# A chain of four graph layers on one core: the two tables that PE reads before each four edge steps joined in one

## The chip, the cores and the metric

The kernel runs on one core of a Trainium2 chip. The metric is the device time of one execution in microseconds (us). Three timed executions took 4398.54, 4406.31 and 4406.6 us; the median is 4406.31 us.

## The reference, cut to what matters

50000 nodes of 128 values pass through four graph layers, with a residual and a layer normalisation after each. There are 25000 edges, sorted by `dst`; `dst` is dense at low node numbers (a uniform draw squared), `src` is uniform. The core of each layer is a sum over edges:

```python
# l0, twice: messages weighted by the edge, summed by dst, averaged, two products, leaky relu
agg = jax.ops.segment_sum(x[src] * ew[:, None], dst, num_segments=n) + x
# l1: rows of dst summed by src
msg_sum = jax.ops.segment_sum(x[col] @ W_msg + b_msg, row, num_segments=n)
# l2: edge attributes summed by dst
aggregated = jax.ops.segment_sum(edge_attr, dst, num_segments=num_nodes)
# l3, twice: rows reflected at a relation's unit vector, summed by dst
h_ref = h_src - 2.0 * dot * h_rel
out = jax.ops.segment_sum(h_ref, tgt, num_segments=x.shape[0])
```

## The kernel before

A front part sorts the edges by their `dst` and by their `src` node and makes tables of the order in which the sums are taken. Then five edge stages, `l0a`, `l0b`, `l1`, `l3a` and `l3b`, alternate with five node stages. All engines meet between two stages (`stage_end`, `stage_begin`).

The nodes stand in 98 groups of 512 (`GROUPS`), the sorted edges in 196 tiles of 128 (`TILES`). A sum over edges is a product: the tile's 128 gathered rows against a matrix of ones and zeros (`hit`, 128 x 512) that says which of the 512 nodes each edge belongs to. A tile whose edges reach over a border of groups takes one step in each of its groups, so a stage has 293 steps (`STEPS`). Rows are split in three bf16 parts (`got`, `rest`, `tail`), so a step is three multiplications (L1554), and in `l0a`, where the edge attributes of `l2` are summed beside, six. Four banks of PSUM hold four groups; ACT copies a finished group out (L1316), clears its bank (L1301) and stores the sums.

The work of a stage runs on all engines at once. POOL gathers rows in batches of four tiles into a ring of sixteen (L719) and waits, before it fills a place again, for the step that last read it, a number that it loads from `ring_tab` (L712). DVE weighs or reflects the rows, splits them (L1103, L1106), and makes the hits (L1071) up to a hundred steps ahead. PE multiplies. Which tile and which group a step has depends on the data, so PE reads them from tables that the front part wrote in SBUF. Steps go in quads of four; there are 74 (`FOURS`). For each quad PE's queue reads eight words of `step_tab` (L1534): four places in the ring and four banks. For every other quad it reads four words of `wait_tab` (L1540): for each of two quads, how many batches of messages must be ready and how many banks cleared. These are masked (L1563, L1564) and waited for, together with the count of hits. Then the quad's steps follow, each with register operations for its addresses (L1554, in PE's queue) ahead of its weight loads and multiplications. The loads for the next quad stand in the queue behind the last multiplication of a quad and before the waits of the next. The order is written out in the program, without a loop:

```python
of = numbers(step_tab, q + 1, 0, 2 * K)      # eight words
if q % 2:
    waits = waits_of(q + 1)                  # four words
```

The tables are filled on DVE in `step_tables` and cleared before (L1011, L1012).

Of the kernel before, what the change touches and what calls it, by code (L numbers as in the profile page):

```python
# [8 lines left out]
I32 = mybir.dt.int32  # L9
U16 = mybir.dt.uint16  # L10
ALU = mybir.AluOpType
ACT = mybir.ActivationFunctionType
AX_X = mybir.AxisListType.X
PE_ENGINE = mybir.EngineType.PE
# [9 lines left out]
K = 4  # L24
ROWS = K * P
GROUPS = -(-N // ROWS)
LAST_NODES = (N - (GROUPS - 1) * ROWS) // K
XROWS = GROUPS * ROWS
TILES = -(-E // P)
FULL_PARTS = E // TILES  # L30
REST = E - FULL_PARTS * TILES
BATCHES = TILES // K
STEPS = GROUPS + TILES - 1
FOURS = -(-STEPS // K)
# [16 lines left out]
IN_RANGE = "the table is built on the chip from counts of tiles and groups, which bound it"  # L51
# [39 lines left out]
def program(nc, t, out):  # L91

    ctx = ExitStack()
    with ctx:
        def sb(name, shape, dt=F32):
            return ctx.enter_context(nc.sbuf_tensor(name, shape, dt))
# [62 lines left out]
        sorted_by = {"dst": sb("sorted_by_dst", [P, TILES, FIELDS], I32)}  # L159
        node_at = {n: sb(f"node_at_{n}", [P, STEPS]) for n in ("dst", "src")}  # L160
        link3 = sb("link3", [3 * K + 3, 8, P], BF16)
        step_tab = {n: sb(f"step_tab_{n}", [1, FOURS, 2 * K], I32) for n in ("dst", "src")}
        wait_tab = {n: sb(f"wait_tab_{n}", [1, FOURS, 2], I32) for n in ("dst", "src")}
        group_tab = {n: sb(f"group_tab_{n}", [1, 104], I32) for n in ("dst", "src")}
        ring_tab = {n: sb(f"ring_tab_{n}", [1, 56], I32) for n in ("dst", "src")}

# [37 lines left out]
        tab_i = front("tab_i", [1, 4, STEPS + 3], I32)  # L204
# [225 lines left out]
        def stage_begin(engine, n):  # L430

            engine.wait_ge(s_stage, ENGINES * n)
# [380 lines left out]
        def _(dve):  # L813
# [126 lines left out]
            def step_tables(name):  # L940

                n = SORTS.index(name)
                dve.tensor_copy(end_row_i[:, :], total_row[name][:, :])
                dve.tensor_copy(end_col_i[:, :], total_col[name][:, :])
                dve.drain()
                dve.tensor_scalar(end_row_i[:, :], end_row_i[:, :], 7, None, ALU.arith_shift_right)
                dve.tensor_scalar(end_col_i[:, :], end_col_i[:, :], 7, None, ALU.arith_shift_right)
                dve.drain()
                dve.tensor_copy(end_row_f[:, :], end_row_i[:, :])
                dve.tensor_copy(end_col[:, 0:1], end_col_i[:, :])  # L950
                dve.drain()
                dve.scalar_tensor_tensor(out=group_tab[name][:, 0:GROUPS], in0=end_row_f[:, :], scalar=1.0, in1=iota_t[0:1, 0:GROUPS],
                                         op0=ALU.add, op1=ALU.add)
                dve.tensor_tensor(end_col[:, 1:2], end_col[:, 0:1], iota_p[0:GROUPS, 0:1], ALU.add)
                dve.tensor_scalar(past_ring[:, 0:BATCHES], iota_t[0:GROUPS, K - 1:K - 1 + TILES:K], end_col[:, 0:1], None, ALU.is_ge)
                dve.drain()
                dve.tensor_scalar(past[:, :], iota_t[0:GROUPS, :], end_col[:, 1:2], None, ALU.is_gt)
                dve.drain().then_inc(s_tab1, 1)
                dve.wait_ge(s_tab2, n + 1)
                dve.tensor_copy(group_at[name][:, :], ps[:, 7, 0:STEPS + 3])  # L960
                dve.tensor_tensor(ring_tab[name][:, 0:BATCHES], ps[0:1, 7, STEPS + 3:STEPS + 3 + BATCHES], iota_t[0:1, K:K + TILES:K], ALU.add)
                dve.drain()
                dve.tensor_tensor(tile_at[:, :], iota_t[:, :], group_at[name][:, :], ALU.subtract)
                dve.drain()
                dve.tensor_scalar(pick0[name][:, :], tile_at[:, 0:STEPS], iota_p[:, 0:1], None, ALU.is_equal)
                dve.tensor_scalar(pick1[name][:, :], tile_at[0:TILES - P, 0:STEPS], iota_p[0:TILES - P, 1:2], None, ALU.is_equal)
                dve.tensor_copy(tab_i[:, 0, :], tile_at[0:1, :])
                dve.tensor_copy(tab_i[:, 1, :], group_at[name][0:1, :])
                dve.drain()
                dve.tensor_scalar(tab_i[:, 2, :], tab_i[:, 0, :], RING - 1, None, ALU.bitwise_and)  # L970
                dve.tensor_scalar(tab_i[:, 3, :], tab_i[:, 0, :], 2, None, ALU.arith_shift_right)
                dve.tensor_scalar(wait_tab[name][:, :, 1], tab_i[:, 1, K - 1:STEPS + 3:K], 1, GROUPS, ALU.add, ALU.min)
                dve.drain()
                dve.tensor_scalar(wait_tab[name][:, :, 0], tab_i[:, 3, K - 1:STEPS + 3:K], 1, BATCHES, ALU.add, ALU.min)
                dve.tensor_copy(step_tab[name][:, :, 0:K], tab_i[:, 2, :].rearrange("a (q j) -> a q j", j=K))
                dve.tensor_scalar(tab_i[:, 0, :], tab_i[:, 1, :], BANKS - 1, None, ALU.bitwise_and)
                dve.drain()
                dve.tensor_copy(step_tab[name][:, :, K:2 * K], tab_i[:, 0, :].rearrange("a (q j) -> a q j", j=K))
                dve.drain()
# [28 lines left out]
            for name in SORTS:  # L1008
                dve.memset(ring_tab[name][:, :], 0)
                dve.memset(group_tab[name][:, :], 0)  # L1010
                dve.memset(step_tab[name][:, :, :], 0)  # L1011
                dve.memset(wait_tab[name][:, :, :], 0)  # L1012
            step_tables("dst")
            dve.wait_ge(s_win, 16 * len(small_loads))
            dve.wait_ge(s_comb, 1)
# [414 lines left out]
        def _(pe):  # L1430
# [66 lines left out]
            def keys_of_tiles(name):  # L1497

                n = SORTS.index(name)
                pe.wait_ge(s_tab3, 2 * n + 1)  # L1500
                pe.transpose(ps[:, 6, 0:P], keys_s[:, 0:P], ident[:, :])
                pe.transpose(ps[0:TILES - P, 6, P:2 * P], keys_s[:, P:TILES], ident[:, :]).then_inc(s_tab4, 1)
# [25 lines left out]
            def edges(name, n):  # L1528
                stage_begin(pe, n)
                s = edge_s[name]  # L1530
                by = WINDOWS[name][0]
                def numbers(table, q, lo, hi):

                    return nc.values_load_multi_w_load_instructions(  # L1534
                        table[by][0:1, q, lo:hi], engines=[PE_ENGINE], min_val=0, max_val=TILES,
                        skip_runtime_bounds_check_because=IN_RANGE)[1]

                def waits_of(q):

                    return nc.values_load_multi_w_load_instructions(  # L1540
                        wait_tab[by][0:1, q:q + 2, :].rearrange("a q f -> a (q f)"), engines=[PE_ENGINE], min_val=0, max_val=TILES,
                        skip_runtime_bounds_check_because=IN_RANGE)[1]

                w = BUFFERS[name]

                def products(i, slot, bank):

                    slot = nc.s_assert_within(slot, 0, RING - 1, skip_runtime_bounds_check_because=IN_RANGE)
                    bank = nc.s_assert_within(bank, 0, BANKS - 1, skip_runtime_bounds_check_because=IN_RANGE)
                    for h in range(1 + w.pair):  # L1550
                        into = ps[:, BANKS * h:BANKS * h + BANKS, :][:, bass.ds(bank, 1), :].rearrange("p a n -> p (a n)")
                        for part in (w.got_hi[h][:, bass.ds(slot, 1), 1:2 * D:2], w.rest_hi[h][:, bass.ds(slot, 1), 1:2 * D:2],
                                     w.tail[h][:, bass.ds(slot, 1), 0:D]):
                            last = pe.matmul(into, part.rearrange("p a d -> p (a d)"), w.hit[:, i % w.hits, :], start=False, stop=False,  # L1554
                                             skip_group_check=True)
                    last.then_inc(s["step"].sem, 1)

                waits = waits_of(0)
                of = numbers(step_tab, 0, 0, 2 * K)
                for q in range(FOURS):  # L1560
                    ready, clear = waits[2 * (q % 2):2 * (q % 2) + 2]
                    pe.wait_ge(*s["hit"](min(K * q + K, STEPS)))
                    pe.wait_ge(s["msg"].sem, ready & 63)  # L1563
                    pe.wait_ge(s["zero"].sem, clear & 127)  # L1564
                    for j in range(min(K, STEPS - K * q)):
                        products(K * q + j, of[j], of[K + j])
                    if q + 1 < FOURS:
                        of = numbers(step_tab, q + 1, 0, 2 * K)
                        if q % 2:
                            waits = waits_of(q + 1)  # L1570
                if name == "l0b":
                    keys_of_tiles("src")

# [182 lines left out]
            def nodes(phase):  # L1756
                phase()
                stage_end(pe)

            edges("l0a", 1)  # L1760
            nodes(d0)
            edges("l0b", 2)
# [32 lines left out]
```

## Time and profile before

| | us |
|---|---|
| median of three timed runs | 4406.31 |
| span of the profiled execution | 4783.9 |
| busy: PE, DVE, POOL, ACT | 3733.3, 3413.8, 2954.6, 2211.2 |
| `l0a`, from 528 to 944 | 416 |
| `l0b`, from 1277 to 1604 | 327 |
| `l1`, from 2002 to 2333 | 331 |
| `l3a`, from 3309 to 3658 | 349 |
| `l3b`, from 3988 to 4336 | 348 |

The times come from runs without a profile; the span is that of one execution under the profiler, from its first instruction to its last, and the only time that is given for that execution. It is 377.6 us above the median. The stretches of the edge stages are read from the times at which L1534 and L1554 start and end; they hold the first waits of a stage and the last stores of the one before. PE's queue (PEldq in the rows) is the engine's own sequence of instructions: register operations and table loads stand there and are not counted as busy time, and the engine's multiplications (PE) and weight loads (PEld) are issued from it.

### The profile page before, as it was taken

How to read it: one execution, taken by the hardware profiler on the slowest of the kernel's cores; microseconds unless marked ns; L12 is line 12 of the kernel's file. 1: busy time of each engine (PE TensorE's matmuls, PEld its weight loads, DVE VectorE, ACT ScalarE, POOL GpSimd, SP SyncE). 2: the span in 40 equal slices, each digit the busy share in tenths (PEclk: the TensorE clock that was granted, in tenths of full speed). 3: DMA queues.
4: the chain of work that ended last, by engine and by line, in shares of the span. 5: the costliest groups of instructions: out<-in, count | busy, mean ns of one | idle time of the engine just before them, and what ended most of it. 6: DMA issues, size and time to landing. Idle time of an engine off the chain costs nothing.

```text
span 4783.9 us, 90087 instructions
## 1 busy us (share of the span) xinstructions
PE 3733.3 (78%) x18662; PEld 2281.7 (48%) x18662; DVE 3413.8 (71%) x13249; ACT 2211.2 (46%) x4608; POOL 2954.6 (62%) x3411
## 2 busy tenths in 40 slices
PE   2155799998778999777899999995678774778776
PEld 1012344477523455422598888894224442234443
DVE  5338965355665577743498988897877888768898
ACT  0000046733225688633366666664145652256666
POOL 4650355366566699866466666664665776656787
PEclk6556899999889999889899999997899997999999
DMA  3340157777524788534555555552456773467776
GB/s 88 99 74 6 53 173 222 251 230 232 168 86 159 246 259 271 175 124 130 170 166 161 167 162 161 161 168 66 122 180 227 235 234 113 147 194 246 226 238 194
DMA packets 536159, 810.98 MB, mean 170 GB/s; under 512 B 129245, under 2 KB 184005, under 8 KB 535709
## 3 DMA queue, kind: packets, MB, share of 16 engines
q1 hardware_dynamic: 318844, 532.13, 35.3%
q10 hardware_dynamic: 162769, 169.41, 10.5%
q0 software_dynamic: 54096, 104.47, 8.0%
q8 instruction: 157, 2.57, 0.2%
q14 instruction: 293, 2.40, 0.2%
HBM read 493.49 MB, written 311.41 MB: 168 GB/s over the span
## 4 chain that ended last, share of the span: by engine, by line
PE 47%; DVE 19%; issue 14%; DVEq 6%; POOL 6%; DMA 3%; another core or an unknown queue 2%; ACT 1%; POOLq 0%; ACTq 0%; SPq 0%; PEldq 0%
PE ps L1554 18%; DVEq L68 5%; DVE stat L1122 4%; PE ps L1719 4%; PE ps L1700 4%; PE ps L1701 4%; DVE hit L1071 3%; PE ps L1487 3%; POOL got L719 2%; PE ps L1679 2%; POOL x2T L734 2%; PE ps L1710 2%; PE ps L1680 2%; DVE mv L1128 2%
## 5 line engine op out<-in xcount | busy, mean ns | idle before, releaser
L754 POOL TENSOR_TENSOR rstd<-vare,neg_half 128x4 f32<-128x4 f32 x686 | 710.3, 1035 | 430.6 <-DVE vare L1135 429.6
L1554 PE MATMUL ps<-hit,got 128*128 128x512 bf16 x1172 | 492.5, 420 | 381.7 <-issue 155.9
L1316 ACT ACTIVATE evac<-ps 128x512 f32<-128x512 f32 x392 | 233.4, 595 | 861.8 <-PE ps L1554 625.3
L719 POOL DMA_INDIRECT got<-nodes_l,sorted_by_dst x392 | 398.2, 1016 | 239.5 <-PE ps L1554 109.8
L1554 PE MATMUL ps<-hit,tail 128*128 128x512 bf16 x1172 | 490.2, 418 | 22.8 <-issue 20.8
L1554 PE MATMUL ps<-hit,rest 128*128 128x512 bf16 x1172 | 491.9, 420 | 20.2 <-issue 18.9
L1163 DVE TENSOR_TENSOR nT<-sums,ps 128x512 f32<-128x512 f32 x392 | 268.9, 686 | 270.8 <-PE ps L1599 100.3
L1301 ACT ACTIVATE ps<-zeros 128x512 f32<-128x512 f32 x588 | 344.3, 598 | 195.0 <-DVEq L428 170.1
L1554 PEld LDWEIGHTS ps<-hit,got 128*128 x1172 | 121.8, 104 | 649.3 <-issue 566.0
L719 POOL DMA_INDIRECT got_pair<-in_x,sorted_by_dst x196 | 203.5, 1038 | 363.5 <-DVEq L428 190.1
L669 POOL DMA_INDIRECT records_by_src<-record,place_src x196 | 201.1, 1026 | 162.0 <-PE ps L1587 90.6
L1338 ACT ACTIVATE aff<-ps,shift,rstd 128x128 f32<-128x128 f32 x784 | 290.6, 448 | 22.1 <-POOL shift L757 22.1
L1736 PE MATMUL ps<-xin,ident 128*128 128x512 f32 x392 | 218.4, 640 | 84.3 <-DVE nT L1163 84.3
L719 POOL DMA_INDIRECT got<-nodes_c,sorted_by_dst x196 | 195.0, 995 | 134.1 <-PE ps L1554 72.7
L1071 DVE TENSOR_SCALAR hit<-node_of,node_at_dst 128x512 bf16<-128x512 f16 x879 | 260.0, 364 | 11.5 <-SPq L428 11.1
L1348 ACT ACTIVATE xT<-ps 128x512 f32<-128x512 f32 x294 | 175.0, 596 | 196.7 <-PE ps L1666 159.4
L719 POOL DMA_INDIRECT got<-nodes_a,sorted_by_src x196 | 195.1, 996 | 108.0 <-issue 53.7
L1740 PEld LDWEIGHTS ps<-w_r,nT 128*128 128x128 f32 x1568 | 211.8, 196 | 98.5 <-issue 98.5
L1103 DVE TENSOR_TENSOR rest<-got 128x512 f32<-128x512 f32 x196 | 136.1, 694 | 171.8 <-DMA got<-nodes_a,sorted_by_src 116.9
L1128 DVE BATCH_NORM_AGGREGATE mv<-stat 128x2 f32<-128x6 f32 x2744 | 230.3, 155 | 34.3 <-issue 1.9
L669 POOL DMA_INDIRECT records_by_dst<-row,place_dst x196 | 191.5, 977 | 101.7 <-issue 101.7
L743 POOL TENSOR_TENSOR aff<-aff,g 128x512 f32<-128x512 f32 x196 | 248.6, 1268 | 4.4 <-issue 2.9
(276 smaller groups left out, 10298.4 us busy)
## 6 DMA issues: line engine op xcount, KB each, us to landing
nodes_l<-xout SPq DMA_DIRECT2D x196, 256.0 KB
xin<-nodes_l SPq DMA_DIRECT2D x196, 256.0 KB
sums<-sums_l SPq DMA_DIRECT2D x196, 256.0 KB
sums_l0a<-evac_pair ACTq DMA_DIRECT2D x98, 256.0 KB
sums_l<-evac_pair ACTq DMA_DIRECT2D x98, 256.0 KB
sums<-sums_l0a SPq DMA_DIRECT2D x98, 256.0 KB
sums_l0b<-evac ACTq DMA_DIRECT2D x98, 256.0 KB
sums<-sums_l0b SPq DMA_DIRECT2D x98, 256.0 KB
```

What stands on the lines that cost most here:

```text
L68: engine.drain()
L669: pool.indirect_dma_start(out=rec_d[name], out_offset=bass.IndirectOffsetOnAxis(ap=place[name][:, k:k + 1], axis=0), in_=of(k), in_offset= ...
L719: pool.indirect_dma_start(out=BUFFERS[name].got[0][:, k % RING, :], out_offset=None, in_=table, in_offset=bass.IndirectOffsetOnAxis(ap=sor ...
L743: pool.tensor_tensor(aff[:, slot, :, :], aff[:, slot, :, :], g3[:, layer:layer + 1, :].to_broadcast([P, K, D]), ALU.mult).then_inc(s["scal ...
L754: pool.tensor_tensor(rstd[:, n, at, :], vare[:, n, at, :], neg_half[:, :], ALU.pow)\
L1071: dve.tensor_scalar(hit[:, i % HITS, :], node_of[:, :], node_at[by][:, i:i + 1], None, ALU.is_equal)\
L1128: dve.bn_aggr(mv[:, n, slot % 4, k, :], stat[:, n, k, :])
L1163: dve.tensor_tensor(nT[:, slot % 4, :], sums[:, slot, :], ps[:, bank + slot % banks, :], ALU.mult).then_inc(s["nT"].sem, 1)
L1301: last = act.activation(ps[:, BANKS * h + g % BANKS, :], zeros[:, :], ACT.Copy)
L1316: act.activation(w.evac[h][:, slot, :], ps[:, BANKS * h + g % BANKS, :], ACT.Copy).then_inc(s["out"].sem, 1)
L1338: last = act.activation(dest[:, slot % ring, k, :], rows[:, slot % rows.shape[1], k, :], ACT.Identity, bias=shift[:, n, at, k:k + 1], scal ...
L1554: last = pe.matmul(into, part.rearrange("p a d -> p (a d)"), w.hit[:, i % w.hits, :], start=False, stop=False, skip_group_check=True)
```

## The change

The four words of `wait_tab` move into `step_tab`: its row of a quad has twelve words instead of eight, of which ten are used, four places, four banks and the quad's own two wait values. PE reads these ten in one load for each quad. `wait_tab` and its clearing are gone; DVE writes the two wait values to columns 9 and 8 of the new rows with the same instructions. The waits, their values and their place ahead of a quad stay as they were.

```diff
-        step_tab = {n: sb(f"step_tab_{n}", [1, FOURS, 2 * K], I32) for n in ("dst", "src")}
-        wait_tab = {n: sb(f"wait_tab_{n}", [1, FOURS, 2], I32) for n in ("dst", "src")}
+        step_tab = {n: sb(f"step_tab_{n}", [1, FOURS, 3 * K], I32) for n in ("dst", "src")}
...
-                dve.tensor_scalar(wait_tab[name][:, :, 1], tab_i[:, 1, K - 1:STEPS + 3:K], 1, GROUPS, ALU.add, ALU.min)
-                dve.drain()
-                dve.tensor_scalar(wait_tab[name][:, :, 0], tab_i[:, 3, K - 1:STEPS + 3:K], 1, BATCHES, ALU.add, ALU.min)
+                dve.tensor_scalar(step_tab[name][:, :, 2 * K + 1], tab_i[:, 1, K - 1:STEPS + 3:K], 1, GROUPS, ALU.add, ALU.min)
+                dve.drain()
+                dve.tensor_scalar(step_tab[name][:, :, 2 * K], tab_i[:, 3, K - 1:STEPS + 3:K], 1, BATCHES, ALU.add, ALU.min)
...
                 dve.memset(step_tab[name][:, :, :], 0)
-                dve.memset(wait_tab[name][:, :, :], 0)
...
-                def numbers(table, q, lo, hi):
+                def numbers(q):
 
                     return nc.values_load_multi_w_load_instructions(
-                        table[by][0:1, q, lo:hi], engines=[PE_ENGINE], min_val=0, max_val=TILES,
-                        skip_runtime_bounds_check_because=IN_RANGE)[1]
-
-                def waits_of(q):
-
-                    return nc.values_load_multi_w_load_instructions(
-                        wait_tab[by][0:1, q:q + 2, :].rearrange("a q f -> a (q f)"), engines=[PE_ENGINE], min_val=0, max_val=TILES,
+                        step_tab[by][0:1, q, 0:2 * K + 2], engines=[PE_ENGINE], min_val=0, max_val=TILES,
                         skip_runtime_bounds_check_because=IN_RANGE)[1]
...
-                waits = waits_of(0)
-                of = numbers(step_tab, 0, 0, 2 * K)
+                of = numbers(0)
                 for q in range(FOURS):
-                    ready, clear = waits[2 * (q % 2):2 * (q % 2) + 2]
+                    ready, clear = of[2 * K:2 * K + 2]
...
                     if q + 1 < FOURS:
-                        of = numbers(step_tab, q + 1, 0, 2 * K)
-                        if q % 2:
-                            waits = waits_of(q + 1)
+                        of = numbers(q + 1)
```

## Rows read from the trace of the kernel before

**Rows 1.** Page, parts 1 and 3: busy us of each engine; a queue's packets, MB.

```profile
PE 3733.3 (78%) x18662; PEld 2281.7 (48%) x18662; DVE 3413.8 (71%) x13249; ACT 2211.2 (46%) x4608; POOL 2954.6 (62%) x3411
...
q8 instruction: 157, 2.57, 0.2%
```

**Rows 2.** Page, part 4: the chain that ended last, by engine and by line.

```profile
PE 47%; DVE 19%; issue 14%; DVEq 6%; POOL 6%; DMA 3%; another core or an unknown queue 2%; ACT 1%; POOLq 0%; ACTq 0%; SPq 0%; PEldq 0%
PE ps L1554 18%; DVEq L68 5%; DVE stat L1122 4%; PE ps L1719 4%; PE ps L1700 4%; PE ps L1701 4%; DVE hit L1071 3%; PE ps L1487 3%; POOL got L719 2%; PE ps L1679 2%; POOL x2T L734 2%; PE ps L1710 2%; PE ps L1680 2%; DVE mv L1128 2%
```

**Rows 3.** Windows: length, busy us of PE, PEld, DVE, ACT, POOL; clock, DMA, GB/s.

```profile
528.00:944.00 416.00, 388.16 (x1769) 174.41 (x1767) 245.49 (x539) 215.56 (x392) 204.01 (x197) 0.97 0.62 195
1277.00:1604.00 327.00, 236.14 (x895) 92.82 (x895) 186.01 (x443) 117.75 (x199) 200.60 (x197) 0.86 0.41 136
...
3309.00:3658.00 349.00, 239.53 (x892) 93.64 (x892) 251.77 (x981) 116.35 (x196) 195.00 (x196) 0.85 0.50 157
```

**Rows 4.** PE's weight loads in time, `l0b`: start us, us; idle us before and releaser.

```profile
1529.53 0.10 PEld L1554 LDWEIGHTS ps<-hit,got 128*128 x1 [0.52 <-issue]
...
1530.01 0.10 PEld L1554 LDWEIGHTS ps<-hit,got 128*128 x1
...
1531.72 0.10 PEld L1554 LDWEIGHTS ps<-hit,tail 128*128 x1
1532.72 0.10 PEld L1554 LDWEIGHTS ps<-hit,got 128*128 x1 [0.90 <-issue]
```

**Rows 5.** PE's register operations by line, `l0b`: count, then ns minimum/median/maximum.

```profile
L1563 PEldq ALU_OP  x74: 3/36/709, 1280.1 to 1600.1; - x74
...
L1564 PEldq ALU_OP  x74: 2/32/708, 1291.0 to 1600.2; - x74
...
L1554 PEldq FUSED_REGOPS  x586: 3/37/1393, 1291.1 to 1600.7; - x196
```

**Rows 6.** Chain by line in 1400:1604, 2045:2333, 3430:3658 and 4108:4336 us.

```profile
by line: PE ps L1554 47.0%; issue 19.6%; POOL got L719 7.5%; DMA got<-nodes_l,sorted_by_dst 7.1%; DMA sums_l0b<-evac 6.8%; ACT evac L1316 3.0%; DVE hit L1071 1.8%; DVE tail L1106 1.7%; DVE got L1085 1.7%; DVE rest L1103 1.7%; ACT ps L1301 1
...
by line: PE ps L1554 53.5%; issue 24.5%; POOL got L719 11.7%; DMA got<-nodes_a,sorted_by_src 5.1%; DVE hit L1071 1.5%; DVE tail L1106 1.4%; DVE rest L1103 1.4%; POOLq L712 0.2%; ACT evac L1316 0.2%; PE ps L1676 0.1%; PE ps L1679 0.1%; POOLq
...
by line: PE ps L1554 50.6%; issue 19.0%; DMA got<-nodes_c,sorted_by_dst 6.9%; POOL got L719 4.7%; ACT evac L1316 3.4%; ACT ps L1301 2.6%; DVE hit L1071 2.4%; DVE prod L1091 2.3%; DVE got L1096 2.3%; DVE rest L1103 1.8%; DVE tail L1106 1.0%;
...
by line: PE ps L1554 46.6%; issue 18.5%; DMA got<-nodes_l,sorted_by_dst 11.6%; POOL got L719 5.8%; DVE hit L1071 3.7%; DVE prod L1091 3.1%; DVE got L1096 3.1%; DVE rest L1103 2.4%; DVE tail L1106 1.3%; DVEq L1099 0.9%; POOLq L712 0.8%; ACT 
```

**Rows 7.** Table loads by line: PE's of eight, of four words, then ACT's.

```profile
L1534 PEldq TENSOR_LOAD <-step_tab_dst x296: 3/592/1931, 530.3 to 4331.6; - x148
...
L1540 PEldq TENSOR_LOAD <-wait_tab_dst x148: 3/334/1022, 529.7 to 4328.8; - x148
...
L1309 ACTq TENSOR_LOAD <-group_tab_dst x100: 304/312/694, 529.7 to 4331.7; - x100
```

**Rows 8.** What PE idled for before L1554, `l0a` whole, then from 600 us: us, times.

```profile
  issue: 40.1, 41
...
  issue: 6.3, 9
```

**Rows 9.** Loads of four words in the late stretches of `l0b`, `l1`, `l3b`.

```profile
L1540 PEldq TENSOR_LOAD <-wait_tab_dst x26: 328/334/707, 1404.0 to 1596.7; - x26
...
L1540 PEldq TENSOR_LOAD <-wait_tab_src x34: 13/334/712, 2045.7 to 2324.9; - x34
...
L1540 PEldq TENSOR_LOAD <-wait_tab_dst x28: 4/392/955, 4115.2 to 4328.8; - x28
```

**Rows 10.** POOL's gathers, 1400 to 1604 us: busy us, mean ns; idle before by releaser.

```profile
L719 POOL DMA_INDIRECT got<-nodes_l,sorted_by_dst x116 | 119.5, 1030 | 63.2 <-PE ps L1554 32.0 <-issue 31.1
```

**Rows 11.** Clearing of `step_tab` on DVE.

```profile
L1011 DVE MEMSET step_tab_dst<- x1: 552/552/552, 192.4 to 192.4; 1x592 int32 x1
```

**Rows 12.** PE's weight loads in time in a slow stretch of `l0b`.

```profile
1427.05 0.10 PEld L1554 LDWEIGHTS ps<-hit,rest 128*128 x1 [1.23 <-issue]
```

## The prediction

> **What bounds the kernel now.** I read the page first, then the chain of waits, then each edge stage by windows, and last the instructions of PE's own queue. The page has PE busiest, 78% of a span of 4783.9 us, and DVE at 71% [rows 1]. A share that high on two engines says only that stages alternate, so the chain of what ended last is the next view: 47% of it is PE, 14% is "issue", and the longest single line is L1554, the edge products, with 18% [rows 2]. L1554 runs in five stretches: 416 us for `l0a`, and from 327 (`l0b`) to 349 us (`l3a`) for the four single stages [rows 3]. In `l0a` (two banks of products per step) PE is busy 388 of 416 us; in `l0b` it is busy 236 of 327 and in `l3a` 240 of 349 us, so there something else holds it. The change touches only what stands between two quads in these five stretches.
>
> What holds it is seen in the order of PE's weight loads around a quad boundary [rows 4]. Inside a quad they follow each other by 0.214 us (eight intervals from 1530.01 to 1531.72); a quad's first one comes after an idle gap of 0.52 us where one table load stands before it (1529.53) and of 0.90 us where two do (1532.72). The releaser is "issue": no semaphore was late, the queue was busy reading registers. The same shows in the waits' own instructions: L1563 and L1564, the masks of the wait values, which carry the waits, last 36 and 32 ns at the median [rows 5].
>
> That holds from about a third of each stage on. In `l0b` from 1400 us on L1554 and issue make 66.6% of the chain, and in the late stretches of `l1`, `l3a` and `l3b` 78.0, 69.6 and 65.1% [rows 6]. The quads before these stretches wait for their first messages, the late ones for PE's queue.
>
> **The change part by part.** *The price of a load.* A load of eight words lasts 592 ns at the median, one of four 334 ns [rows 7] (296 and 148 of them by the `dst` tables, and a quarter as many more by `src`). The difference, 258 ns for four words, is 64.5 ns a word, which leaves 334 - 4 x 64.5 = 76 ns that each load costs whatever its length. ACT's loads of four words, 312 ns, fit the same price [rows 7]. Between a load and the next instruction of the queue lie a further 58 ns: the second load adds 0.90 - 0.52 = 0.38 us to the gap [rows 4], and 0.38 is 0.334 with some 0.05 to 0.06 around it.
>
> *Removed*: 37 loads of four words in each of five stages, 185 in all. *Added*: two words to each of the 370 loads. Over two quads the words stay twenty (8 + 8 + 4, then 10 + 10), so what goes is one load's fixed part: 76 + 58 = 134 ns. By lengths: before 592 + 592 + 334 + 3 x 58 = 1692 ns, after 2 x (592 + 129 + 58) = 1558 ns. Every boundary then costs about 0.65 us of idle PE, where now 0.52 and 0.90 alternate.
>
> No load of ten words is in this trace. Bounds from the nearest rows: not under the 592 ns of eight words (then two quads would save 134 + 258 = 392 ns), and not over the price of an eight and a four one after the other, 592 + 334 = 926 ns (two quads then lose 276 ns). I take 721 ns, the line through both lengths, since both lie in one plain transfer of a row of the same tile and no row shows a step.
>
> *Where it counts.* In `l0a` a quad is 24 multiplications and PE's idle time there ahead of L1554 is 40.1 us by issue over the whole stage, but only 6.3 us from 600 us on [rows 8]; the loads run while the multiplications of the last quad still execute. I cost it at nothing there; with that cover gone it would be 37 x 0.134 = 5 us. In the early stretches of the other four the saved time turns into a longer wait for messages: nothing. In the four late stretches stand 26, 34, 28 (`l3a`, whose row is not shown) and 28 of the four-word loads [rows 6, 9], 116 in all: 116 x 0.134 = 15.5 us. Of these I count the share in which L1554 and issue are the chain, on the mean of the four 70% [rows 6]: 10.9 us. In the rest the ring of gathered rows, DVE's splitting or the stores of the sums are last, and follow PE only in part.
>
> *What is late next.* POOL gathers a batch ahead of PE. In `l0b`'s late 204 us it is busy 119.5 us and loses 31.1 to its own issue, 32.0 to PE [rows 10]; so the gathers could end some 32 us sooner if PE let them, nine times the 26 x 0.134 = 3.5 us that the change wants there.
>
> *No cost.* The clearing of two `wait_tab` goes, the clearing of the two `step_tab` grows from 592 to 888 words, at 552 ns for 592 by under 0.28 us each [rows 11]: at most 0.6 us in the front part, less what goes. The writes of the two columns are the same instructions to another stride. The waits keep their values and their places ahead of each quad; none is added, nothing is moved past another queue. The tables take 1184 bytes more of a partition (2 x 74 x 8), which shifts the buffers behind them and changes no access.
>
> *Fewer instructions.* PE's queue now and then crawls: around 1427 us a weight load inside a quad stands behind 1.23 us of idle time, one of four alike within six us, with issue as the releaser [rows 12], and register operations that take 37 ns at the median reach 1.4 us in that stage [rows 5]. The trace has 157 packets of 2.57 MB in an instruction queue [rows 1]. 185 fewer instructions can spare one such crawl, at most some 6 us; I leave it out of the sum and in the range. The Trainium skill (Runtime: NRT & Kernel Launch, section Instruction fetch mechanics) gives 16 KiB blocks of 256 instructions, which by it would be 0.7 of one block here; the trace's 2.57 MB over 157 packets agree with the block's size.
>
> The sum is made in the profiled execution, of which only the span is given, 4783.9 us, and that is 377.6 us above the median of the three timed runs, 4406.31. If the crawls belong to profiling, the timed run is nearer to the gathers' own pace and a part of the 10.9 us goes. If the late stretches shrink in proportion, the saving per load stays, since it is a fixed time of PE's queue. I keep 11 us: 4406.3 - 10.9 = 4395.4, say 4395.
>
> **The rivals.** *Hidden after all, no change.* Without crawls PE's queue needs 3.19 us from quad to quad with two loads (1529.53 to 1532.72) and 0.38 less, 2.81 us, with one [rows 4], 0.75 us a step, against 2.57 us of multiplications (12 x 0.214), while POOL needs 4 x (1.03 + 0.27) = 5.2 us for a batch of four tiles [rows 10]. A batch takes four to eight steps, so where fewer than 5.2 / 0.75, some seven, fall to it POOL or the DMAs set the pace, and what PE saves becomes its wait. For it: 377.6 us of the profile's span are not in the timed runs, and gathers stand in every late chain with 12 to 17%, DMA and POOL together [rows 6]. Against it: POOL's 32.0 us of waiting for PE. Price: 15.5 x 0.2 = 3 us gained, so 4401 to 4408.
>
> *The price lies in the words alone.* Then twenty words before and after cost the same: 4406. The two lengths speak against it: four words at 64.5 ns would be 258, not 334 ns. The Trainium skill (Runtime: NRT & Kernel Launch, section Instruction fetch mechanics) has such a rule, about 200 ns per register even in bulk, for register loads from HBM. These are from SBUF and the trace disagrees in size: 592 ns for eight where the rule would give 1600.
>
> *Slower: the long load has a step.* If a load over eight words is done as two reads, each boundary costs 926 ns instead of 592: a pair of quads rises from 1692 to 2 x (926 + 58) = 1968 ns, 276 ns more, and 116 of them 32 us: 4438. It decides from 1692/2 - 58 = 788 ns on, only 67 ns above my 721. For it: ten words and a stride of twelve are new here, the third length no row shows; loads already stretch at times, to 1931 ns at most [rows 7], and a longer one has more to be stretched. Against: the regular price of two lengths.
>
> **How the numbers follow.** The forecast's case (a fixed part goes, PE's queue is what is late) has 0.50, with its own range 4380 to 4400; hidden 0.30; words alone 0.07; the step or a stretched load 0.13, from 4410 up. Three timed runs spread over 8 us, so 0.2% (8.8 us) is about what can be told from no change. The forecast's case puts a few in a hundred within it, and hidden and words nearly all theirs: faster 0.47, same 0.39, slower 0.14. The low end is the 15.5 us in full, 7 us for the stretching that goes with the second load (its median in the last stage is 392 ns, not 334 [rows 9]) and one crawl of 6 us: 4378. The high end goes a quarter of the way into the step: 4413.
>
> **What would show it.** PE's queue with 370 loads of some 720 ns and none at `wait_tab`; gaps of 0.6 to 0.7 us ahead of every late quad; `l0a` as long as before; the four single stages each 2 to 5 us shorter; POOL's waits for PE down by as much. Wrong would be: loads of 790 ns or more; gaps gone but longer waits at L1563 or L1564; stages of one length while something outside of them moved.

## The result

The changed kernel takes 4418.57 us (median of five, 4413.81 to 4422.76) against 4403.33 us for the kernel before (five, 4393.41 to 4406.6): a ratio of 1.0039, interval 1.0026 to 1.0051. It is slower by 0.4%. I had forecast 4395 us, in a range of 4378 to 4413. Two executions of the later comparisons, one of before at 11224 us and one of the twelve-word kernel at 5523 us, are left out of their ratios.

The page of the profile after; PE is busy for 82% of a span shorter than that of [rows 1]:

```profile
span 4421.0 us, 89900 instructions
...
PE 3611.1 (82%) x18662; PEld 2252.9 (51%) x18662; DVE 3415.3 (77%) x13247; ACT 2213.6 (50%) x4608; POOL 2978.8 (67%) x3411
...
q8 instruction: 157, 2.57, 0.2%
...
PE 45%; DVE 18%; POOL 12%; issue 12%; DVEq 6%; DMA 5%; ACT 1%; POOLq 1%; ACTq 0%; SPq 0%
PE ps L1546 14%; DVEq L68 5%; POOL got L718 4%; DVE stat L1120 4%; PE ps L1708 4%; POOL records_by_dst L668 4%; PE ps L1689 4%; PE ps L1690 4%; DVE hit L1069 3%; PE ps L1668 2%; PE ps L1610 2%; PE ps L1609 2%; PE ps L1699 2%; PE ps L1669 2%; POOL x2T L733 2%
```

The span, 4421.0 us, agrees with the timed runs. That of the first profile of before, 4783.9 us, did not. Of [rows 1] the order of the engines stayed, PE and DVE busiest, and the 157 packets of code. So the kernel before was run and profiled once more.

**e0_before**, the same text as before.

> The kernel before once more, for a profile that stands nearer to its timed runs than the first one (span 4783.9 us against a median of 4403 us), whose PE queue crawled some sixty times. All theories expect a span of 4395 to 4410 us, loads of 592 ns (eight words) and 332 ns (four), and no register operation of L1554 over 0.6 us. Stages then: l0b 295 us, l1 280, l3a 305, l3b 305, each 3 to 6 us under the changed kernel's. If the crawls come back, they belong to the kernel and not to that one execution.

Measured: 4402.95 us, span 4401.1 us. The crawls of PE's queue did not come back: no register operation of the products takes more than 89 ns in this profile (L1554), nor more than 84 in the changed kernel's (L1546), where [rows 5] had up to 1393. The changed kernel's first mask of the wait values is its L1554. Columns as there; first before, with its loads of eight and of four words, then the changed kernel:

```profile
L1554 PEldq FUSED_REGOPS  x3223: 37/55/89, 388.6 to 3950.2; - x190
...
L1534 PEldq TENSOR_LOAD <-step_tab_dst x296: 587/592/1605, 375.6 to 3949.0; - x148
...
L1540 PEldq TENSOR_LOAD <-wait_tab_dst x148: 327/334/1027, 375.0 to 3946.2; - x148
```

```profile
L1554 PEldq ALU_OP  x370: 36/36/36, 375.6 to 3969.7; - x185
...
L1546 PEldq FUSED_REGOPS  x3223: 37/55/84, 387.9 to 3970.2; - x190
```

There are two levels. The first three comparisons had the kernel before near 4403 us, the four later ones had it at 4776 to 4819 us, as in the first profile. Within one comparison, which is on one chip, the level didn't change. But the record names the same chip, number 10, for one comparison at 4403 us and for two at 4781 and 4811, so the chip alone doesn't set the level, though the expectations below speak of slow chips. The 383 us between the two profiles of before stand in a few places: 155 in the front part, 49 between `l0a` and `l0b`, and 37 to 51 in each of the four single stages. `l0a`, `d2` and the rest differ by at most 2.2 us each. At the slower level 228 of PE's 9500 register operations last over 0.3 us, most of them some 0.7 us, 156 us together; in the second profile there are none. They aren't waits for code, as some expectations below have it: between two packets of code, at 1421.8 and 1445.4 us, six of them start from 1423.5 to 1428.4. In the single stages the mean of PE's granted clock is 0.87 or 0.88 there, against 0.91 to 0.96 in the second profile. Whether that comes from the pauses or from what sets the level isn't shown, and what sets it stays open. All comparisons of traces below use this second profile of before.

**Where the time went.** The changed kernel's loads, in place of [rows 7]:

```profile
L1532 PEldq TENSOR_LOAD <-step_tab_dst x296: 1072/1087/2263, 374.2 to 3968.2; - x148
L1532 PEldq TENSOR_LOAD <-step_tab_src x74: 1071/1082/1578, 1773.6 to 2052.0; - x74
```

Ten words take 1087 and 1082 ns at the median, not 721. The gaps ahead of a quad's first weight load, in place of [rows 4], first in the changed kernel, then in the second profile of before:

```profile
1326.73 0.10 PEld L1546 LDWEIGHTS ps<-hit,got 128*128 x1 [1.34 <-issue]
...
1330.01 0.10 PEld L1546 LDWEIGHTS ps<-hit,got 128*128 x1 [1.00 <-issue]
...
1333.28 0.10 PEld L1546 LDWEIGHTS ps<-hit,got 128*128 x1 [0.99 <-issue]
```

```profile
1303.32 0.10 PEld L1554 LDWEIGHTS ps<-hit,got 128*128 x1 [1.12 <-issue]
...
1306.23 0.10 PEld L1554 LDWEIGHTS ps<-hit,got 128*128 x1 [0.62 <-issue]
...
1309.53 0.10 PEld L1554 LDWEIGHTS ps<-hit,got 128*128 x1 [1.02 <-issue]
...
1312.34 0.10 PEld L1554 LDWEIGHTS ps<-hit,got 128*128 x1 [0.52 <-issue]
```

Where gaps of 1.12 or 1.02 us alternated with 0.62 or 0.52, 1.34, 1.00 and 0.99 follow each other. For the length of the edge stages I take the first and the last start of a stage's `got` products, `l0b` and `l3a`, first in before, then in the changed kernel:

```profile
L1554 PE MATMUL ps<-hit,got x293: 376/379/635, 1085.6 to 1358.0; 128*128 128x512 bf16 x147
...
L1554 PE MATMUL ps<-hit,got x293: 376/379/635, 3031.8 to 3318.1; 128*128 128x512 bf16 x147
```

```profile
L1546 PE MATMUL ps<-hit,got x293: 376/379/634, 1087.8 to 1371.7; 128*128 128x512 bf16 x147
...
L1546 PE MATMUL ps<-hit,got x293: 376/379/634, 3032.1 to 3327.5; 128*128 128x512 bf16 x147
```

The last two times before the semicolon are the starts: `l0b` 272.4 us before and 283.9 after, `l3a` 286.3 and 295.4. Read so, all five stages and, in `d2`, PE's last products:

| | before (second profile) | changed | difference |
|---|---|---|---|
| `l0a` | 395.6 | 397.0 | +1.4 |
| `l0b` | 272.4 | 283.9 | +11.5 |
| `l1` | 264.0 | 268.6 | +4.6 |
| `l3a` | 286.3 | 295.4 | +9.1 |
| `l3b` | 282.7 | 293.3 | +10.6 |
| last products of `d2` | 922.7 | 905.7 | -17.0 |

The edge stages lose 37.2 us, the node stage `d2`, of which the change touches no line, gives 17.0 back; 20.2 us together, and the spans differ by 19.9, the medians of the timed runs by 15.2. Each column is one profile, but they repeat: the four single stages sum to 1105.4 us here and to 1105.2 and 1105.4 in two further kernels with the loads of before (e3 and e2, below), to 1141.2 in the changed kernel and 1141.6 in e4, which has its loads. `d2`'s row comes from these, L1719 in before and L1708 in the changed kernel; the second line has what the products alone waited for by issue, in us, how often, and the longest:

```profile
L1719 PE MATMUL ps<-w_o,hidT x1568: 273/275/582, 2084.8 to 3007.5; 128*128 128x128 f32 x196
...
PE ps L1719 <- issue: 21.0, 8, 3.0
```

```profile
L1708 PE MATMUL ps<-w_o,hidT x1568: 272/275/553, 2102.2 to 3007.9; 128*128 128x128 f32 x196
...
PE ps L1708 <- issue: 10.4, 4, 2.7
```

The products' pauses by issue fall from 21.0 us in 8 places to 10.4 in 4. The loop has five passes, so it returns four times: two pauses at each return before, one after. At one return they look so, before and then after (start, length, idle time before):

```profile
2301.20 1.02 PE L1719 MATMUL ps<-w_o,hidT 128*128 128x128 f32 x7 [2.57 <-issue]
2304.68 1.65 PE L1719 MATMUL ps<-w_o,hidT 128*128 128x128 f32 x6 [2.47 <-issue]
```

```profile
2318.63 3.56 PE L1708 MATMUL ps<-w_o,hidT 128*128 128x128 f32 x16 [2.63 <-issue]
```

Two pauses of 2.6 and 2.5 us, seven products apart, against one. The two kernels' schedules of these products part at the four returns alone, by 3.3, 3.7, 3.7 and 5.9 us, 16.6 in sum: more than the pauses' 10.6, the rest isn't broken down. With each pause stands a packet of code. Counted in ten microseconds around a return, 2298 to 2308 us before, 2315 to 2325 after (packets, MB, share):

```profile
q8 instruction: 3, 0.05, 1.9%
```

```profile
q8 instruction: 2, 0.03, 1.3%
```

Each packet has 16384 bytes. Away from the returns they start 12 to 20 us apart in the loop, but at this return at 2298.6, 2302.4 and 2306.2 us before, and at 2315.9, 2319.8 and 2325.6 after. All twelve pauses, eight before and four after, begin within 0.6 us of a packet's start and end 1.3 to 1.9 us after its end. In the changed kernel the second of the close packets comes without a pause.

### The profile page after: what moved, and what is told of

Its sections match the earlier page's. It is cut to its first block, busy times and chain, and to the rows that moved or that the text cites. A ratio compares the mean times of both kernels' runs of the same rounds, so it can differ in the third digit from the quotient of the medians.

```text
span 4421.0 us, 89900 instructions
## 1 busy us (share of the span) xinstructions
PE 3611.1 (82%) x18662; PEld 2252.9 (51%) x18662; DVE 3415.3 (77%) x13247; ACT 2213.6 (50%) x4608; POOL 2978.8 (67%) x3411
## 4 chain that ended last, share of the span: by engine, by line
PE 45%; DVE 18%; POOL 12%; issue 12%; DVEq 6%; DMA 5%; ACT 1%; POOLq 1%; ACTq 0%; SPq 0%
PE ps L1546 14%; DVEq L68 5%; POOL got L718 4%; DVE stat L1120 4%; PE ps L1708 4%; POOL records_by_dst L668 4%; PE ps L1689 4%; PE ps L1690 4%; DVE hit L1069 3%; PE ps L1668 2%; PE ps L1610 2%; PE ps L1609 2%; PE ps L1699 2%; PE ps L1669 2%; POOL x2T L733 2%
## 5 line engine op out<-in xcount | busy, mean ns | idle before, releaser
L1546 PE MATMUL ps<-hit,got 128*128 128x512 bf16 x1172 | 466.4, 398 | 370.2 <-DVE hit L1069 201.3
L1546 PE MATMUL ps<-hit,rest 128*128 128x512 bf16 x1172 | 467.0, 398 | 0.0
L1546 PE MATMUL ps<-hit,tail 128*128 128x512 bf16 x1172 | 466.3, 398 | 0.0
L1546 PEld LDWEIGHTS ps<-hit,got 128*128 x1172 | 118.5, 101 | 624.4 <-issue 528.1
L668 POOL DMA_INDIRECT records_by_src<-record,place_src x196 | 216.3, 1104 | 97.8 <-issue 56.1
L668 POOL DMA_INDIRECT records_by_dst<-row,place_dst x196 | 202.7, 1034 | 103.6 <-issue 103.0
L1546 PE MATMUL ps<-hit_pair,got_pair 128*128 128x512 bf16 x586 | 224.6, 383 | 25.1 <-DVE hit_pair L1069 14.5
```

What stands on the lines that cost most here:

```text
L668: pool.indirect_dma_start(out=rec_d[name], out_offset=bass.IndirectOffsetOnAxis(ap=place[name][:, k:k + 1], axis=0), in_=of(k), in_offset= ...
```

## The experiments

**e1_lengths.** What does a load cost by its length? Loads of each length were put behind PE's last work:

```diff
+            for at in (0, 1, 2, 3):
+                nc.values_load_multi_w_load_instructions(flat[0:1, 12 * at:12 * at + 10], engines=[PE_ENGINE], ...)
```

> The kernel before with 52 more table loads on PE after its last work: 1 to 12 and 16 words from step_tab, each length four times, starting 0, 12, 24 and 36 words into the table. Theory A, the step is in the length: 64.5 ns a word up to eight (205 ns for two, 463 for six), and a jump of some 350 to 430 ns between eight and nine, with ten at 1084 ns and all four starts alike. Rival B, the step is in the stride of twelve words, the start of a row off 32 bytes: the starts at 12 and 36 words cost more than those at 0 and 24 for lengths under nine too, and ten words from the start of the table 721 ns. Rival C, a neighbour on the chip stretches long loads: ten words cost 721 ns here, where nothing else runs.

Measured: 4404.06 us, and not one of the added loads in the trace. Nothing used their values, and the build left them out. Nothing follows on the lengths.

**e1b_lengths.** The same with the values used:

```diff
+                got = nc.values_load_multi_w_load_instructions(flat[0:1, 12 * at:12 * at + 10], ...)[1]
+                use(got)
```

`use` adds the values up, and the sum chooses the bank of one small product.

> The first try at lengths showed none of its loads, as nothing used their values. Now each load's values are added up and choose the bank of one small multiplication, behind the end of the last stage's normalisation: 1 to 12 and 16 words of step_tab, each length from words 0, 12, 24 and 36. Theory A, the step is in the length: 64.5 ns a word to eight (205 ns for two, 463 for six, 592 for eight), a jump of some 350 to 430 ns between eight and nine, ten at 1084 ns, all four starts alike. Rival B, a start off 32 bytes costs: 12 and 36 dearer than 0 and 24, ten words from word 0 at 721 ns. Rival C, neighbours stretch long loads: ten words cost 721 ns here, where little else runs.

Measured, ns as minimum, median, maximum of four loads (starts at words 0, 12, 24, 36), for 1 to 12 and for 16 words:

```profile
L1782 PEldq TENSOR_LOAD <-step_tab_dst x4: 298/306/342, 4394.9 to 4396.7; - x4
...
L1786 PEldq TENSOR_LOAD <-step_tab_dst x4: 531/533/538, 4397.3 to 4400.1; - x4
...
L1790 PEldq TENSOR_LOAD <-step_tab_dst x4: 763/764/766, 4401.0 to 4404.5; - x4
...
L1794 PEldq TENSOR_LOAD <-step_tab_dst x4: 333/333/339, 4405.7 to 4408.0; - x4
...
L1798 PEldq TENSOR_LOAD <-step_tab_dst x4: 578/584/602, 4408.8 to 4411.9; - x4
...
L1802 PEldq TENSOR_LOAD <-step_tab_dst x4: 815/822/827, 4412.9 to 4416.7; - x4
...
L1806 PEldq TENSOR_LOAD <-step_tab_dst x4: 1054/1058/1062, 4418.0 to 4422.6; - x4
...
L1810 PEldq TENSOR_LOAD <-step_tab_dst x4: 588/593/598, 4424.1 to 4427.3; - x4
...
L1814 PEldq TENSOR_LOAD <-step_tab_dst x4: 838/846/850, 4428.4 to 4432.4; - x4
...
L1818 PEldq TENSOR_LOAD <-step_tab_dst x4: 1072/1082/1084, 4433.7 to 4438.5; - x4
...
L1822 PEldq TENSOR_LOAD <-step_tab_dst x4: 1315/1316/1321, 4440.1 to 4445.6; - x4
...
L1826 PEldq TENSOR_LOAD <-step_tab_dst x4: 843/848/853, 4447.4 to 4451.9; - x4
...
L1830 PEldq TENSOR_LOAD <-step_tab_dst x4: 1102/1106/1107, 4453.4 to 4458.9; - x4
```

Theory A had the place of the jump wrong: it is not at eight words. A load costs about 76 ns, 257 for each whole four words, and for every single word left over about 230 where no whole four stands in the load, 241 to 253 on the mean behind whole fours. Four words take 333 ns and three take 764, and nine (846) are cheaper than ten. Twelve take 848 ns, less than ten at 1082. Rivals B and C fall: the four starts lie within 24 ns of each other (44 for one word) at every length, and ten words cost 1082 ns where PE has nearly no other work. My two points, four and eight words, were both whole fours.

**e2_before_145, e3_shift, e4_after_111.** Why is `d2` shorter? What the three change:

```diff
+            for _ in range(145):
+                pe.sem_inc(s_bm, 1)
...
+        unused = sb("unused", [1, 2 * FOURS, 2], I32)
```

The first edit is e2's, on before; e4 has it with 111 on the changed kernel. The last line is e3's, on before.

> The kernel before with 145 semaphore increments put at the head of PE's program, where PE waits for the first tables anyway. The changed kernel's edge stages are 37 to 40 us longer than in the fresh profile of before, but its node stage d2 is 19 us shorter (963 against 982 us), and PE's pauses ahead of the last products of d2 come once per pass of its loop instead of twice. Theory P: the 111 PE instructions that the change takes out ahead of that loop move its first instruction within the blocks of 256 instructions in which code is fetched, from place 232 to place 121 (counted in the compiled programs); 145 more instructions put it at 121 too. P expects d2 at 963 us, one pause a pass, and 4403 - 19 = 4384 us. Rival S: the tables are 1184 bytes larger and shift the buffers behind them; then d2 stays at 982 us and the time at 4403. Edge stages as before under both.

> The kernel before with an unused buffer of 1184 bytes behind wait_tab, so that all later buffers lie where the changed kernel has them; PE's program is that of before to the instruction. Theory P: 4403 us, d2 982 us with two pauses a pass. Rival S: 4384 us, d2 963 us.

> The changed kernel with 111 semaphore increments at the head of PE's program, which put the first instruction of d2's loop back to place 232 of its block. This takes away what d2 gave back and leaves the price of the loads: theory P expects 4418 + 19 = 4437 us, d2 at 982 us, edge stages as in the changed kernel (l0b 297, l1 281, l3a 310, l3b 307 us). Rival S: 4418 us, d2 963 us.

Measured: e2 4388.31 us, ratio to before 0.9974 (0.9963 to 0.9984); e3 4402.02 us, 0.9999 (0.999 to 1.0009); e4 4437.0 us, 1.0082 (1.0064 to 1.01). The last products of `d2` in e2, e3, e4, and their waits by issue as above:

```profile
L1721 PE MATMUL ps<-w_o,hidT x1568: 273/275/550, 2083.8 to 2990.2; 128*128 128x128 f32 x196
...
PE ps L1721 <- issue: 10.2, 4, 2.8
```

```profile
L1720 PE MATMUL ps<-w_o,hidT x1568: 273/275/582, 2078.6 to 3000.3; 128*128 128x128 f32 x196
...
PE ps L1720 <- issue: 20.6, 8, 3.3
```

```profile
L1710 PE MATMUL ps<-w_o,hidT x1568: 273/275/582, 2099.0 to 3021.1; 128*128 128x128 f32 x196
...
PE ps L1710 <- issue: 20.1, 8, 2.8
```

They last 906.4, 921.7 and 922.1 us, with 4, 8 and 8 pauses. (The expectations' 982 and 963 us are those of the whole stage.) Theory P holds three times, rival S falls: 145 instructions that do nothing make the kernel before faster, by 15 us by the medians and 0.26% by the ratio, the buffers' place makes nothing, and 111 such instructions take from the changed kernel what `d2` gave it. e4 is the price of the loads alone: 4437.0 against 4403.47 us, 0.8%. The runs show that the number of instructions ahead of the loop decides: with the loop's start at place 232 of a block of 256, as counted in the compiled programs, 24 instructions are left to the next block and a second pause comes seven products on; at 121 there is none. By the Trainium skill (Runtime: NRT & Kernel Launch, section Instruction fetch mechanics) code is fetched in blocks of 256 instructions, and a taken branch whose target lies outside the current window of two blocks waits until the target has been fetched. The trace agrees: a packet of 16384 bytes stands with each of the pauses.

**e5_twelve to e5d_twelve.** One edit to the changed kernel:

```diff
-                        step_tab[by][0:1, q, 0:2 * K + 2], engines=[PE_ENGINE], ...
+                        step_tab[by][0:1, q, 0:3 * K], engines=[PE_ENGINE], ...
```

> The changed kernel with one edit: PE's load reads the whole row of twelve words, two of them unused. The lengths measured alone give 76 ns, 257 ns for each whole four words and 237 ns for each word left over, so twelve (848 ns) are cheaper than ten (1084). Theory A (whole fours): loads of 848 ns, a mean of 0.906 us between two quads against 1.142 in the changed kernel and 0.846 before. From before to the changed kernel with d2's loop put back, 0.296 us a quad cost 34 us (4403 to 4437), 115 us for each us; so 0.060 us cost 7 us, and d2's loop stands where it does in the changed kernel and gives its 15 us: 4403 + 7 - 15 = 4395 us. Rival D, what costs is a load over eight words whatever its remainder, or the register writes: then 4418 us or more. l0b 287, l1 277, l3a 302, l3b 299 us by A.

> The twelve-word kernel again. Its first comparison ran on a chip on which the kernel before takes 4776 us, as the first profile of before (4783.9 us) had it, not the 4403 us of the other chips; there PE waits some sixty times for its code. On a chip of 4403 us theory A expects 4395 us (loads 848 ns: 7 us more than before; d2's loop: 15 us less), rival D 4418 us. If it is the slow chip again, a ratio of 0.995 once more.

> Twelve words, one edit from the changed kernel: each load 236 ns shorter. Theory A: 23 to 27 us under the changed kernel on any chip, so 4395 us on one of 4403 us and a ratio of 0.995 to 0.997 on a slow one.

> Twelve words. On a chip of 4403 us theory A says 4395 us, rival D 4418. On a slow chip the ratio of 0.997 again, which would leave the other chips' case open.

All four were in comparisons at the level of about 4800 us. Ratios to before there: 0.9952 (0.9935 to 0.9969), 0.9968 (0.9951 to 0.9986), 0.9975 (0.9958 to 0.9992) and 0.9969 (0.9949 to 0.9988). Most of that gain is the loop's, not the loads': `d2`'s last products take 904 to 909 us in the four traces, against 921.8 in the first profile of before, and those 13 to 18 us are 0.3 to 0.4% of 4800. What loads of twelve words alone do against before was timed at neither level.

**e6_twenty to e6d_twenty, and e7_twenty_222, e7c_twenty_222.** Twenty words, five whole fours, for two quads; e7 has 222 idle instructions ahead in addition, which put `d2`'s loop back to place 232:

```diff
-        step_tab = {n: sb(f"step_tab_{n}", [1, FOURS, 3 * K], I32) ...
+        step_tab = {n: sb(f"step_tab_{n}", [1, FOURS, 2 * K + 2], I32) ...
...
-                        step_tab[by][0:1, q, 0:2 * K + 2], engines=[PE_ENGINE], ...
+                        step_tab[by][0:1, q:q + 2, :].rearrange("a q f -> a (q f)"), engines=[PE_ENGINE], ...
...
-                    if q + 1 < FOURS:
+                    if q % 2 and q + 1 < FOURS:
                         of = numbers(q + 1)
```

> Rows of ten words, two rows read in one load of twenty words ahead of every other quad; 37 loads a stage and no others. By the law of whole fours 76 + 5 x 257 = 1361 ns and 58 around it, a mean of 0.710 us a quad, 0.136 under before: this is the saving of fixed parts that the change was meant for, without its remainders. At 115 us for each us: 16 us less; 222 fewer PE instructions ahead of d2's loop put its start to place 10 of a block, one pause a pass: 15 us less. Theory A: 4403 - 16 - 15 = 4372 us. Rival E, only the uneven boundaries count: 1.42 us at one and nothing at the next leaves PE starved at the one and bound by its own multiplications at the other, so half the gain is lost: 4380 us. Rival F, long loads stretch under traffic (the ten-word loads had a mean of 1246 ns at a median of 1084): 4388 us.

> The twenty-word kernel again. Theory A, on a chip of 4403 us: 4372 us, loads of 1361 ns at the median. Rival E, uneven boundaries give half back: 4380 us. Rival F, long loads stretch under traffic (1553 ns at the median on the slow chip): 4388 us, the gain of d2's loop alone.

> The twenty-word kernel with 222 semaphore increments at the head of PE's program, which put d2's loop at place 232 of its block as in the kernel before: what is left is the price of the loads alone. Theory A 4403 - 16 = 4387 us; rival E 4395; rival F 4403. d2 at 982 us under all.

> Twenty words for two quads. Theory A 4372 us on a chip of 4403 us; rival E (uneven boundaries) 4380; rival F (stretched long loads) 4388. On a slow chip 0.994 to 0.995, as in both runs so far.

> Twenty words with d2's loop put back to place 232: the loads alone. Theory A 4387 us on a chip of 4403 us; rival E 4395; rival F 4403. On a slow chip 0.998 to 0.999.

> Twenty words for two quads. On a chip of 4403 us theory A says 4372 us, rival E 4380, rival F 4388. On a slow chip 0.995 again.

Ratios to before: e6 0.9947 (0.9934 to 0.9961), 0.9944 (0.9926 to 0.9963), 0.9961 (0.9943 to 0.9978) and 0.9928 (0.9895 to 0.9961); e7 0.9989 (0.9972 to 1.0006) and 1.0 (0.9981 to 1.0019). So twenty words in one load beat the kernel before by 0.4 to 0.7% each time, and the changed one too (e6c 0.9961, e8 1.0018 in the same comparison), but nearly all of the gain on before is the loop's place: `d2`'s last products take 906 us in the four traces of e6 and 922 in both of e7. What is left, the fixed parts saved, which was the intent of the change, brings nothing that could be measured at this level, though PE's loads last 276 to 279 us together in e7's traces and 316 in the first profile of before. The interval of e7 does not exclude the 11 us of my forecast, a ratio of 0.9977; that of e7c ends just above it.

**e8_changed**, the changed kernel beside the others:

> The changed kernel again, on one chip with the three below. Theory A on a chip of 4403 us: 4418 us; on one of 4776 to 4820 us, where more of PE's time goes to waiting for code, about the ratio 1.002 to 1.004. A rival on which the slow chips hide the loads: 0.997, the gain of d2's loop alone.

Measured: 1.0018 (0.9999 to 1.0036), in one comparison with e5c, e6c and e7c. From ten words to twelve, with nothing else changed, the ratio falls from 1.0018 to 0.9975, 0.4%, some 21 us by the ratios and 12 by the medians: more words, less time. The loads of e8, of e5c and of e6c:

```profile
L1532 PEldq TENSOR_LOAD <-step_tab_dst x296: 3/1103/2348, 529.2 to 4343.2; - x148
```

```profile
L1532 PEldq TENSOR_LOAD <-step_tab_dst x296: 3/851/1969, 539.8 to 4347.4; - x148
```

```profile
L1532 PEldq TENSOR_LOAD <-step_tab_dst x148: 3/1571/2869, 528.7 to 4322.8; - x148
L1532 PEldq TENSOR_LOAD <-step_tab_src x37: 218/1362/1822, 2016.0 to 2336.1; - x37
```

Twelve words take 851 ns here, the law's 848. Of twenty, the `src` tables have 1362 ns as expected, the `dst` tables 1571, so the stretching that rival F named is there in one of the two tables; its times were for the other level and weren't measured.

## Why the prediction was wrong

**The price of a load: the step that failed.** I drew a line through the loads of four and eight words, took 721 ns for ten and gave 592 to 926 ns as bounds. It is 1084 ns (the middle of 1087 and 1082), outside both, and my own sign of being wrong, loads of 790 ns or more. 64.5 ns a word was right only within whole fours; each of the two left over costs 247. Two quads cost 2 x (1084 + 58) = 2284 ns instead of 1692, a loss of 592 ns where I had a gain of 134. The upper bound came from the nearest rows, but a load of two words was not among them: 592 + 533 (two words, alone) is 1125 ns and would have held it.

**The rival "the long load has a step"** (0.13) was the right side, and its time of 4438 us is e4's 4437.0, but by chance: it took 276 ns for two quads and let all of it reach the end in 116 places. Shown is 0.296 us a quad over the 296 quads of the four single stages, 88 us, of which the stages lost 35.8 us (the table without `l0a`), 41%.

**Where it counts.** Late in a stage the changed kernel's gap is the load and its surroundings, as forecast, and `l0a` hid it: +1.4 us. The share of 70% of the 116 late pairs of quads was too high for a loss: 116 x 0.592 is 68.7 us, and 35.8 us are 52% of it; for a saving no share could be measured. [rows 10] had POOL waiting 32.0 us for PE in late `l0b`; in the second profile of before it is 6.2 us, in the changed kernel 15.1:

```profile
L719 POOL DMA_INDIRECT got<-nodes_l,sorted_by_dst x128 | 128.3, 1003 | 41.5 <-issue 35.4 <-PE ps L1554 6.2
```

```profile
L718 POOL DMA_INDIRECT got<-nodes_l,sorted_by_dst x130 | 130.8, 1006 | 51.2 <-issue 36.1 <-PE ps L1546 15.1
```

In the kernel before, at 4403 us, the gathers nearly keep their own pace: 1003 ns and 277 of issue each, 5.1 us for a batch. From this I argue that a longer load pushes PE behind them while a shorter one could hardly draw them forward, the case "hidden after all". That isn't shown. At 4403 us the shorter loads weren't timed. At 4800 us, where e7's 0.9989 and 1.0 were measured, POOL did wait 32.0 us for PE, so the gathers' pace doesn't explain them; PE's register operations crawl there, and e7's loads from the `dst` tables last 1608 ns at the median, not the 1361 of the law. The chain of the changed kernel in its late `l0b` has L1546 and issue at 47.7%, where [rows 6] had L1554 and issue at 66.6%:

```profile
by line: POOL got L718 28.6%; PE ps L1546 24.9%; issue 22.8%; DMA got<-nodes_l,sorted_by_dst 10.8%; DVE hit L1069 2.7%; DVE tail L1104 2.3%; DVE rest L1101 2.3%; DVE got L1083 2.3%; ACT evac L1314 1.4%; ACT ps L1299 1.0%; POOLq L711 0.6%; A
```

**Fewer instructions.** I priced 185 fewer at one crawl, read in `l0b`, at most 6 us, and left it out of the sum. They gave 17 us, in `d2`, since the 111 of them that stand ahead of its loop moved the loop's start. The packets of code stayed 157, and the crawls weren't waits for code. The sign of such a term is chance: in e2 145 more ahead of it gave 15 us. So the measured 4418.57 us is the sum of two misses: the loads cost some 34 us (e4), and the loop gave half of it back.

**The sum against the median.** I noted that the profile's span stood 377.6 us above the timed runs and kept its late stretches all the same. The doubt was right: PE's slack, POOL's waits and the chain's shares of [rows 3, 6, 10, 12] belonged to an execution at the other level. The prices of the loads in [rows 7] did not: 592 and 334 ns came back. What the second load adds to a gap, 0.38 us in [rows 4], is 0.50 us in both pairs of the second profile.

Right were the removal of 37 loads a stage, the fixed part of 76 ns and the wait values' operations, which stayed as short as 36 ns. By this law the changed kernel is over two quads 134 ns cheaper in fixed parts, as forecast, and 4 x (247 - 64.5) = 730 ns dearer in words left over: 596 ns, and the medians in the traces give 592.

## What to carry to other kernels

Read table words into registers in whole fours, padding where need be: twelve cost 848 ns, ten 1082; four cost 333, three 764. A line through two sizes says nothing of a third with another remainder. When a change takes instructions out of an unrolled program, look at the loops behind it too: here the place of one loop in the code was worth some 15 us, though no line of it was changed. And a profile whose span lies 9% off the timed runs is to be taken again before its slack is used.

## What the runs showed of the hardware

The price of a load of table words into PE's registers: 306 ns for one word, 533 for two, 764 for three, 333 for four, and from there again a climb of 234 to 253 for each further word, back down to 593 at eight and 848 at twelve (e1b). PE's loop in `d2`, with its start 24 instructions ahead of a block's end, pauses twice at each return, 2.6 and 2.5 us; with 135 to go it pauses once (e2, e4). A packet of 16384 bytes in the instruction queue stands with each pause. The same program takes 4403 us in some comparisons and 4776 to 4819 in others; the loads' medians are the same in both (592 and 334 ns), and at the slower level 228 of PE's 9500 register operations last over 0.3 us, up to 1393 ns [rows 5], where the products' take 89 at most in the other.
